# Extra TensorE products on idle PSUM banks in six waits of an attention, MLP and Fourier-filter kernel

## The reference

```python
# layer 0: attention with relative positions, 12 heads of 16, then an MLP
attn = q @ k.T * scale + rel_h + rel_w ; attn = softmax(attn) ; x = shortcut + (attn @ v) @ proj_w + proj_b
x = x + gelu(layernorm(x) @ mlp_w1 + b1) @ mlp_w2 + b2
# layer 1: a filter in the Fourier domain, then a second MLP
h = layernorm(x)
xf = rfft2(h)                       # along W, then along H
o1 = relu(cmul(xf, w1) + b1) ; o2 = softshrink(cmul(o1, w2) + b2)     # complex, 8 blocks of 24
x = x + h + irfft2(o2)
x = x + gelu(layernorm(x) @ fc1_w + b) @ fc2_w + b
```

## Time and profile before

| what | us |
|---|---|
| median of 3 runs | 1165.86 (1165.65 to 1169.21) |
| the profiled execution, its own time | 1164.59 |
| its span, from the first to the last instruction | 1162.5 |
| PE busy | 1023.6 (88%) |
| DVE busy | 856.3 (74%) |
| ACT busy | 704.9 (61%) |
| mean granted TensorE clock | 0.923 of full |

### The profile page before, as it was taken

One profiled execution on the slowest core, in us unless ns is written; L12 is line 12 of the kernel. 1 busy time (PEld: TensorE's weight loads), 2 busy tenths in 40 slices (PEclk: granted clock), 3 DMA queues, 4 the chain that ended last, 5 costly groups with the idle time before them and its releaser, 6 DMA issues.

```text
span 1162.5 us, 35977 instructions
## 1 busy us (share of the span) xinstructions
PE 1023.6 (88%) x15434; PEld 731.4 (63%) x15434; DVE 856.3 (74%) x1702; ACT 704.9 (61%) x1008; POOL 190.6 (16%) x159
## 2 busy tenths in 40 slices
PE   4867588999999999999999999999888864984997
PEld 2545135666677777776767777776476644762776
DVE  3847687999999999999999999996256761232442
ACT  3646136777777777777877778777844430322554
POOL 2540009000000000000000000000265650001443
PEclk9985568999999999999999999999998876995999
DMA  7498697846566574756556566563000001111110
GB/s 119 126 249 266 199 171 115 137 89 110 91 104 104 92 122 82 127 86 110 93 103 117 91 104 106 90 110 72 18 22 22 21 11 47 39 51 44 35 40 21
DMA packets 83338, 109.13 MB, mean 94 GB/s; under 512 B 14349, under 2 KB 75569, under 8 KB 82996
## 3 DMA queue, kind: packets, MB, share of 16 engines
q1 hardware_dynamic: 82660, 105.17, 47.0%
q10 hardware_dynamic: 528, 1.77, 1.2%
HBM read 85.47 MB, written 21.44 MB: 92 GB/s over the span
## 4 chain that ended last, share of the span: by engine, by line
PE 70%; DVE 8%; DMA 7%; issue 6%; ACT 4%; POOL 3%; SPq 1%; ACTq 1%; POOLq 0%; DVEq 0%
PE ps L1026 35%; PE ps L1177 17%; PE ps L1021 16%; DVE mx_p L1467 3%; DVE xh L104 2%; POOL hid L748 2%; DVE stage_lo L1439 1%; ACT hid L943 1%; DMA mask<-in_c_mask 1%; DMA m_d<-mneg 1%; DMA rel_d<-stage_lo 1%; ACT hid_f L949 1%; PE ps L1126 1%; POOL rstd L112 1%; PE ps L1034 1%
## 5 line engine op out<-in xcount | busy, mean ns | idle before, releaser
L1467 DVE TENSOR_REDUCE mx_p<-ps 128x1 f32<-128x464 f32 (+1 forms) x1080 | 608.0, 627 | 42.1 <-PE ps L1026 31.9
L896 ACT ACTIVATE prob<-ps 128x768 f32<-128x768 f32 x648 | 496.0, 810 | 192.4 <-PE ps L1026 191.9
L1026 PE MATMUL ps<-kc,qc 112*32 112x464 f16 (+1 forms) x4320 | 463.7, 370 | 14.8 <-DMA qc<-rel_d 11.6
L1026 PE MATMUL ps<-qv,ka 113*32 113x384 f16 x5184 | 406.0, 328 | 12.5 <-issue 5.1
L1177 PE MATMUL ps<-prob,v_ext 128*32 128x384 f32 x2592 | 294.2, 487 | 1.4 <-issue 0.9
L1026 PEld LDWEIGHTS ps<-qv,ka 113*32 113x32 f16 x5184 | 217.7, 97 | 88.5 <-issue 27.2
L1026 PEld LDWEIGHTS ps<-kc,qc 112*32 112x32 f16 x4320 | 176.1, 96 | 112.5 <-issue 31.4
L1177 PEld LDWEIGHTS ps<-prob,v_ext 128*32 128x32 f32 x2592 | 118.8, 111 | 15.6 <-issue 2.4
L1021 PE MATMUL ps<-w_dn,hid 128*96 128x192 f16 x864 | 83.2, 261 | 7.7 <-ACT hid L943 7.7
L1021 PEld LDWEIGHTS ps<-w_dn,hid 128*96 128x96 f16 x864 | 80.5, 133 | 14.3 <-ACT hid L943 8.8
L721 POOL COPY v_ext<-v_all 128x288 f32<-128x288 f32 x12 | 5.1, 430 | 514.7 <-PE ps L1177 514.7
(11 more groups left out here) (104 smaller groups left out, 853.8 us busy)
## 6 DMA issues: line engine op xcount, KB each, us to landing
qv<-rel_d SPq DMA_DIRECT2D x216, 144.0 KB
qv<-kq_d SPq DMA_DIRECT2D x108, 216.0 KB
qc<-rel_d SPq DMA_DIRECT2D x24, 216.0 KB, 4.2
xin<-in_x SPq DMA_DIRECT2D x12, 288.0 KB, 3.6
kq_d<-khl SPq DMA_DIRECT2D x24, 144.0 KB, 2.3
q_h<-kq_d SPq DMA_DIRECT2D x9, 288.0 KB, 4.9
q_w<-qw_d SPq DMA_DIRECT2D x9, 288.0 KB, 7.1
rel_d<-stage_hi SPq DMA_DIRECT2D x4, 648.0 KB, 8.0
```

The lines of the kernel that those rows point to most:

```text
L896: nc.scalar.activation(prob[:, s4(p, s), :].rearrange("p (a b) -> p a b", a=2), ps[:, 3 + 2 * (s % 2):5 + 2 * (s % 2), 0:CW], ACT.Exp).the ...
L1026: ins = nc.tensor.matmul(ps[c:c + 32, bank, 0:w], l[:, c:c + 32], r, start=True, stop=True, tile_position=(0, c))
L1467: nc.vector.tensor_reduce(mx_p[:, q * GT + k // MP, k % MP:k % MP + 1], ps[:, slot, 0:min(MW, N - k % MP * MW)], AX, ALU.max).then_inc(uni ...
```

## The change

A new helper issues `count` products of a 128-column matrix with 384 moving columns of the same operand, into a bank that nobody reads. They wait for nothing of their own, signal nothing, and no result is used. Calls of it stand at seven points of PE's program, around six waits.

```diff
+            def stay_awake(count, bank, x):
+
+                for _ in range(count):
+                    mm(ps[:, bank, 0:CW], x[:, 0:128], x[:, 0:CW])
...
+            stay_awake(22, 7, kc[0:HD + 2 * S, 0, :])
             period(0, 0)
...
             pe.wait_ge(u_ok, NC - 1)
+            stay_awake(34, 4, hid[:, 0, 0, :])
             dft(NC - 1)
+            stay_awake(44, 4, hid[:, 0, 0, :])
...
                 layer2(g)
+            stay_awake(14, 3, hid[:, 0, 0, :])
             inverse(G - 1)
+            stay_awake(42, 3, hid[:, 0, 0, :])
...
             inverse_w(0)
+            stay_awake(30, 3, hid[:, 0, 0, :])
             norm_transposed(0, ln4, t4_ps)
+            stay_awake(8, 3, hid[:, 0, 0, :])
             chunks(pe, block1)
```

## The result

The changed kernel takes 1159.43 us (median of 20 runs, 1153.3 to 1163.91) against 1165.38 us of before (20 runs, 1163.66 to 1169.23). The ratio, estimated from the same runs, is 0.9943, with a 95% interval of 0.993 to 0.9956: 6.6 us or 0.57% faster (the two medians alone lie 5.95 us apart). The seven calls fill seven waits: one at the first maxima, and six late ones. The profiled execution took 1158.64 us, with a span of 1156.5, against 1164.59 and 1162.5.

A forecast was written before the change was run, and what follows sets the result against it. PE's chain of short steps runs at half clock after waits; full clock gives 10.7 us, the first maxima lose 1.5, sum 9.2: 1156.2 us taken. Forecast 1153 to 1159, with the partial case and costlier maxima 1152 to 1161.5.

The forecast's parts named there:

- the first maxima: Start of head 0: 22 added products delay the scores about 3.3 us, 1.85 comes back; net 1.5 us lost.
- the late part: Last product down of the first MLP to the last product: full clock in its steps gains 10.7 us.
- The products fit: Six late waits: at full clock each set ends 0.5 to 1.9 us before its wait does, delaying nothing.
- The eight steps: Last W transform to `inverse_w(1)`: eight steps at full instead of half clock give 0.38 to 1.90 us each, 10.7 together.
- So I expect 1.00 from the end of the first MLP to the end: Late waits: pauses left are shorter than a 2.2 us one the clock survived, so it stays full.
- The partial rival: Clock lost in some waits, placed ahead of the last W transform: total gain 5.7 us, 1160; chance 0.17.
- the full 34: Set ahead of the last W transform: 34 products take 5.5 us in a wait of 7.40.
- the 44: Set ahead of `transform(0)`: 7.2 us in a wait of 7.85; if the clock falls before it, 2.1 late.
- the 22: Products added at the first maxima, begun at half clock: 18 cold and 4 warm, scores 3.3 us late.
- the stop: Head 0, PE's 3.52 us for "issue", read as waiting for instructions: stays; work pushed behind it costs 1.2 to 2.0 us.
- The slower rival: Late waits: added products do not hold the clock and overshoot; 21.5 us lost, 1186; chance 0.04.

The follow-up runs named there:

- filter_hold: The changed kernel with 6 more products between the first group's transform and its `layer1`, where PE waits for `f_x`: 1157.33 us, ratio 0.9916.
- late_hold: The changed kernel without the 22 products at the first maxima, with 6 more ahead of `layer1(0)`: 1154.2 us, ratio 0.9894.
- mlp_fill: late_hold with products added in the waits of the first MLP, 16 in chunks 1 to 4, 32 in chunk 5: 1147.08 us, ratio 0.9835.
- best: mlp_fill with 42 instead of 34 products ahead of the last W transform: 1148.36 us, ratio 0.9873.
- weights_late: The changed kernel with the four MLP weight loads issued some 20 us later, behind head 0's second-part loads: 1161.99 us, ratio 0.9965.
- late_only: The changed kernel without the 22 products at the first maxima; the six later sets stay: 1157.89 us, ratio 0.9922.
- narrow: late_only with each added product cut to 32 weight columns, still 384 moving columns: 1156.3 us, ratio 0.9931.
- overshoot: late_only with 60 instead of 34 products ahead of the last W transform: 1157.97 us, ratio 0.9932.
- after: The changed kernel itself, first measurement, against before: 1159.43 us, ratio 0.9943.
- after_again: The changed kernel, unchanged, timed and profiled once more: 1157.07 us, ratio 0.9924.

## Why the prediction was right, and where it was off

It was right in direction and range: 1159.43 lies in 1152 to 1161.5, and the gain of 6.6 us by the ratio stands against 9.2 forecast (8.9 when it was timed again). In the profiles 6.0 us were gained: the late part gave 1.9 less than forecast, the first maxima and what follows cost 0.4 more, and 0.8 lies ahead of everything that was changed.

- *The products fit.* Each late product took 0.163 us at full clock, and in the changed kernel's profile all six late sets ended 0.5 to 1.8 us ahead of what PE waited for.
- *The eight steps.* Seven came as forecast within 0.1 us: 1.53, 1.91, 1.86, 1.50, 0.86, 2.12 and 1.46. The one that failed is the 1.86 for `layer1(0)`, which gave 0.2 (5.00 against 5.21), and in a second profile cost 1.3. The step behind it is "So I expect 1.00 from the end of the first MLP to the end", with the reason that no pause left is as long as the 2.2 us that the clock had survived. In the changed kernel the clock survived the pause of 1.79 and fell in `layer1(0)`, behind a pause of 1.06. From 985.5 to 989.2 PE is busy for only 2.05 of 3.70 us, with two pauses and the twenty small products of `transform(0)` between them. Six products in the second pause kept it, in four kernels of four, while without them it was kept in two of seven. Whether the first pause or the small products alone would do the same was not tried. With them the late part takes 181.3 us in filter_hold and 180.9 in late_hold (181.9 and 181.4 in mlp_fill and best), a gain of 10.4 to 10.8: the forecast 10.7 was the right sum of what is to be had, and the change leaves about 2 to 4 of it.
- *The partial rival* (a pause in which the clock is lost) is what happened, at another place than I put it. Its own place, ahead of the last W transform, lost the clock too, but in one profile of nine with the full 34 (mlp_fill), and there the 44 made `transform(0)` 0.9 us late, where I had 2.1.
- *The first maxima.* The loss of 1.5 us stands against 1.9 in the profiles and a mean of 1.4 over the twelve kernels; since single profiles scatter by more, that the 22 cost this much is consistent with the runs and not shown. And it agrees in size, not in its working. The 22 products were to take 6.4 us and took 5.7, since the clock rose sooner; the scores started 2.5 us late and not 3.3; the work that ran cold took 3.4 us warm and not 3.9. So of the 1.5 us that were to be left at this point nothing is (9.0 us after the last maximum in both kernels), and that the total fits is luck: the 2 us come later, behind the stop. What I said of the stop was half right. It does come from the loads of PE's instructions: it moves by 22 products with 22 products ahead of it, full or tiny, as the prediction had it. But I took it to be what bounds head 0's start in the changed kernel as well, and there it shrank to 0.44 us and a wait of 5.9 us for `qv<-m_d`, 91 products on, took its part, with its stretch at half clock behind it. weights_late shows the cause of the latter, full DMA engines; late_only has it without the 22, so that what decides between the two stops stays open. The Trainium skill's rule ("Runtime: NRT & Kernel Launch", Instruction fetch mechanics), that crossing a block is mostly hidden, holds in the late waits, where no stop for issue shows, and not in head 0, where the measured 3.5 us decide.
- *The slower rival.* Its doubt was whether these products hold the clock, for products of 32 columns had run at 0.50. narrow settles that: width alone is not what matters. What else sets the maxima apart (four side by side, 464 moving columns, DVE's pace) was not tried. Its price was right in kind: overshoot measures 2.3 us, where 60 products of 0.163 us in a wait of 7.3 give 2.5. The rule of the Trainium skill ("TensorE: Matmul & The Clock Gate", Step-by-step: what each phase is for) that products leave in program order agrees.

## What to carry to other kernels

Where a chain of short steps runs through TensorE with waits of some microseconds between them, price each step at both clocks from rows of the same trace, and count products that end just before each wait does: eight steps had 10.7 us in them here (the change got 8.8 of them, six more products nearly all), and the same in the first MLP gave 7 to 10.5 more. Look at the steps between the pauses too, not only at the longest pause: small products with pauses of 0.59 and 1.06 us on their sides lost the clock in five profiles of seven, a single pause of 1.79 us in one of nine. Where the next wait is set by full DMA queues, filling a wait ahead of it bought nothing that could be measured.

## What the runs showed of the hardware that was not expected

- Products of 32 weight columns and 384 moving columns hold the clock at 1.00 (narrow, 20.2 us at 1.00 through the sets and their pauses), while the maxima, four sets of 32 columns side by side at 464 moving columns and 99% busy by the trace, run at 0.50 for 24.7 us, in every profile. The share of busy time in the trace does not tell these two apart. DVE's pace sets that of the maxima, one unit in 0.55 us.
- The clock's fall at one place is not fixed: with the same program it was at 0.50 for 3.4 and for 6.8 us around `layer1(0)` (after, after_again), and for 10.2 in late_only; against 3.32 us at full clock `layer1(0)` took 1.7 to 3.2 us more.
- With the DMA engines full, PE stopped for 3.2 to 4.1 us at a place that moves with the count of its own instructions (3.52 in before, 3.24 in narrow, 4.06 in best, each behind 261 products of head 0).
- Behind 2.3 MB of weight loads, 9.5 us passed from the issue of the 1.5 KB write to `m_d` to the issue of the read back (after), and 1.2 us with these loads moved (weights_late).
